# Half of a depthwise convolution moved from TensorE to VectorE, and the row maxima spread three to two over the making of the inputs

## The chip, the cores and the metric

The kernel runs on one core of a Trainium2 chip. The metric is the device time of one execution in microseconds (us), lower is better. Before the change it is 1499.34 us, the median of three runs (1496.52 to 1502.08).

## What is computed

A sequence of 2048 rows of 128 channels passes through two layers. Layer 0 is a complex exponential filter along the sequence (done as a scan) and a gated token mix. Layer 1 has a state-space block ("mamba") in two directions, forward and backward, an attention with 16 heads of 8 channels, and eight experts. The change touches the inputs of the state-space block and what lies beside their making:

```
xz = einsum('bld,ed->ble', x, Win)            # 256 channels u, 256 channels z
u, z = split(xz)
uc = depthwise_conv(u, convw, 4 taps, causal) + convb
u  = silu(uc)
dtr, Bm, Cm = split(einsum('bld,ed->ble', u, Wx))      # 8 + 16 + 16
dt = softplus(einsum('blr,dr->bld', dtr, Wdt) + bdt)
h  = exp(dt * A) * h + (dt * u) * B ;  y = h . C + u * D ;  y = (y * silu(z)) @ Wout
```

The attention is softmax(q k^T / sqrt(8)) v. The kernel takes the row maximum of the scores in a pass of its own (scores in bf16 pieces on TensorE, a maximum over each 128x512 block on VectorE), and a second pass computes the scores again, transposed and with the maximum folded in, takes the exponential on ScalarE and weighs v with it.

## The kernel before

The program has three stages with a barrier between them: `layer0_stage`, `front_stage` (queries, keys, values, the inputs of the state-space block, the whole attention) and `tail_stage` (the state-space scan, the experts). Only the front is changed, and some loads of its weights in `layer0_stage` (L140), which fetch the four taps for 256 channels.

**The chunks.** The state-space inputs are made in NN = 8 chunks n of 512 positions, four forward and four backward, each in two halves b of 128 channels. A step is one bank of PSUM written by TensorE and emptied by ScalarE; four banks (`prep`) go round. Steps are "U" (n, b), "Z" (n, b), "X" n, "D" (n, b). The order `STEPS` (L511 to L522) is: U and Z of chunks 0 and 1; then, for each pair p of chunks, U and Z of pair p+1 and X and D of pair p. A U step is four accumulating matmuls (L887) over the normed input `xm` shifted by 0 to 3 positions, each with weights W_in times a tap (`S.taps`, made once by GpSimd, L620): the convolution is inside the projection. Z is one matmul, X two (contracting u), D one with 8 rows of contraction.

**ScalarE** empties the banks in the same order (`empty`, L692): U with silu and bias to `u`, Z with silu to `z`, X as a copy to `bcx`, D as |x| to `soft` and relu to `dt`. After each pair's D steps `softened` (L719) takes exp and log1p of `soft`. Each change of function costs a table load. Then come the 256 units of the attention, two exponentials of 128x1024 each (L744).

**VectorE** makes `xm` (`normed_input`, L806; it waits for the last Z step of chunk n-2), adds the two parts of the softplus (`softplus`, L817), and takes the row maxima (`maxima`, L761: a job is two heads, so two reductions of 128x512, L768). Jobs are numbered: 32 for each of 16 attention steps. `LEAD` = 10 jobs beyond the first 32 are done before the units begin; two more jobs stand in every unit until all 512 are done. After job 31 the maxima are turned (`turn_max`, L918) and written as rows (`place_rows`, L777).

**TensorE** runs STEPS[0:16] alone (values are made after the first four), and then one step and one job's two matmuls in turn (L978 to L983), 42 times; 40 steps lie in there. The maxima's PSUM banks are a ring of three: the two matmuls of job n wait until the first reduction of job n-1 is done (L913). A unit (L984) is two scores, a job, the weighing of the unit before, a job.

**SyncE** issues all DMAs in the order of L570 to L609: the stores of the q and k pieces, `store_uz` of chunks 0 and 1 (u as soon as ScalarE has emptied it, then z), 32 loads of q and k for the first group of heads, `store_uz` 2 and 3, then for p = 0, 1: `store_bc`, `store_dt`, `store_dtu` of pair p and `store_uz` of pair p+2; then `place_max(0)` (the rows of maxima); then `store_bc`, `store_dt`, `store_dtu` of pairs 2 and 3. ScalarE may overwrite `z` of chunk n only when the store of z of chunk n-2 has landed (L703), and `bcx` of chunk n only when the store of `bcx` of chunk n-2 has landed (L707).

**GpSimd** multiplies dt by u (`scaled_input`, L623) and splits the maxima into bf16 pieces (`split_max`).

## Time and profile before

| | |
|---|---|
| median of three runs | 1499.34 us (1496.52 to 1502.08) |
| the profiled execution | 1494.55 us, of which 1492.8 us are the span of its instructions |
| TensorE, matmuls | 994.9 us busy (67%) |
| VectorE | 1241.4 us busy (83%) |
| ScalarE | 865.8 us busy (58%) |
| GpSimd | 514.5 us busy (34%) |
| granted TensorE clock, mean of the span | 0.819 of 2.4 GHz |

The span falls into five stretches: layer 0 and the making of q and k to 115.9 us; the 16 steps that TensorE makes alone to 153.9 us; steps and jobs in turn, and the log and exp of the last pair, to 261.6 us, where ScalarE starts its first attention exponential; units with jobs to 871 us, and units without to 913.4 us; the tail stage to the end.

An engine's busy share over the whole span does not say which one sets the end of a stretch. For that the rows further down give starts, durations and, in square brackets, the idle time before a group of instructions and who ended it. A matmul of 32-bit data appears as two records. Ends of matmuls are modelled, so the step from one start to the next is the better measure.

### The profile page before, as it was taken

The page shows a single profiled execution, that of the slowest core. Times are in us where ns is not written, and L with a number is a line of the kernel's source. Part 1 is how long each engine was busy: PE and PEld are TensorE (multiplying, and loading weights), DVE is VectorE, ACT ScalarE, POOL GpSimd, SP SyncE. Part 2 cuts the span into 40 slices and gives each one's busy share as a digit, 9 for nine tenths or more (in the row PEclk, how much of TensorE's full clock was granted, in tenths as well). Part 3 has the DMA queues.
Part 4 walks back from the last instruction along what each step waited for, and adds up shares of the span by engine and source line. Part 5 has one row for each costly group of instructions (what it writes and reads, how often), then busy time and mean ns, then how long its engine had stood idle before and what let it go on. Part 6 is the DMA issues. An engine that isn't in the chain of part 4 may idle for free. (4 is left out here: it accounts for less than half of the span.)

```text
span 1492.8 us, 18241 instructions
## 1 busy us (share of the span) xinstructions
PE 994.9 (67%) x5865; PEld 327.3 (22%) x5865; DVE 1241.4 (83%) x1874; ACT 865.8 (58%) x1286; POOL 514.5 (34%) x472
## 2 busy tenths in 40 slices
PE   1439997888888888888888886243275555542444
PEld 0124331111111111111111112021043333310111
DVE  7975466899999999999999932899996666798996
ACT  3134557677777777777777786243454444553441
POOL 2311021300000000000000000698995666799894
PEclk7769996899999999999999998555566767675555
DMA  3004242300000000000000003764857675795530
GB/s 88 0 3 159 107 171 107 105 13 1 1 26 26 1 1 7 21 25 2 1 1 2 1 1 73 165 134 102 199 122 172 143 171 139 169 188 112 113 85 29
DMA packets 88785, 111.42 MB, mean 75 GB/s; under 512 B 15539, under 2 KB 46042, under 8 KB 88690
## 3 DMA queue, kind: packets, MB, share of 16 engines
q1 hardware_dynamic: 87666, 108.16, 29.1%
q0 software_dynamic: 1024, 2.10, 0.5%
q8 instruction: 47, 0.77, 0.2%
q14 instruction: 48, 0.39, 0.1%
HBM read 84.36 MB, written 25.56 MB: 74 GB/s over the span
## 5 line engine op out<-in xcount | busy, mean ns | idle before, releaser
L768 DVE TENSOR_REDUCE at_mpart<-psum 128x1 f32<-128x512 f32 x1024 | 637.8, 683 | 52.5 <-PE psum L915 49.2
L744 ACT ACTIVATE at_probs<-psum 128x1024 f32<-128x1024 f32 x512 | 495.2, 1021 | 147.3 <-PE psum L943 147.0
L1276 POOL TENSOR_TENSOR t_inject<-t_dus,t_bs 128x512 f32<-128x512 f32 x256 | 320.1, 1276 | 93.3 <-issue 38.9
L1642 PE MATMUL psum<-t_hc,stack 128*32 128x512 f32 x512 | 108.2, 930 | 254.5 <-DVE t_hc L1454 254.3
L956 PE MATMUL psum<-at_probs,at_vg 128*32 128x512 f32 x2048 | 274.7, 608 | 0.5 <-ACT at_probs L744 0.4
L915 PE MATMUL psum<-at_ks,at_qs 56*128 56x512 bf16 x1024 | 203.1, 393 | 94.0 <-DVE at_mpart L768 93.3
L1334 ACT ACTIVATE psum<-t_dts,aneg 128x512 f32<-128x512 f32 x256 | 175.9, 692 | 83.5 <-DVE t_hc L1454 39.3
L640 POOL CAST at_m<-at_mneg 128x16 bf16<-128x16 f32 x16 | 3.1, 196 | 584.3 <-DVE at_mneg L773 572.7
L1531 DVE TENSOR_TENSOR_SCAN psum<-psum,t_last,t_inject 128x512 f32<-128x512 f32 x142 | 178.8, 1277 | 11.9 <-issue 9.5
L943 PE MATMUL psum<-at_qs,at_ks 59*128 59x512 bf16 x1024 | 157.8, 380 | 9.7 <-ACT at_probs L744 8.2
L915 PEld LDWEIGHTS psum<-at_ks,at_qs 56*128 56x128 bf16 x1024 | 49.3, 93 | 424.2 <-DVE at_mpart L768 408.5
L1346 ACT ACTIVATE t_last<-psum 128x1 f32<-128x1 f32 x142 | 24.2, 171 | 175.6 <-DVE t_hc L1454 175.3
L1454 DVE TENSOR_TENSOR t_hc<-psum,t_cs 128x512 f32<-128x512 f32 x186 | 124.0, 667 | 0.0
L1531 DVE TENSOR_TENSOR_SCAN t_hp<-psum,t_last,t_inject 128x512 f32<-128x512 f32 x50 | 63.4, 1269 | 36.9 <-issue 24.2
L1263 POOL TENSOR_TENSOR t_hc<-t_hp,t_cs 128x512 f32<-128x512 f32 x70 | 88.8, 1269 | 15.2 <-DVE t_hp L1531 15.1
L1642 PEld LDWEIGHTS psum<-t_hc,stack 128*32 128x32 f32 x512 | 14.5, 133 | 316.6 <-issue 300.3
L943 PEld LDWEIGHTS psum<-at_qs,at_ks 59*128 59x128 bf16 x1024 | 50.7, 96 | 60.1 <-ACT at_probs L744 30.6
L888 PE MATMUL psum<-mp_xm,mp_taps 128*128 128x512 f32 x128 | 62.9, 642 | 0.0
L626 POOL TENSOR_TENSOR mp_u<-mp_soft_dt,mp_u 128x1024 f32<-128x1024 f32 x8 | 22.2, 2798 | 107.0 <-DVE mp_soft_dt L820 107.0
L1637 PE MATMUL psum<-t_uz,diag 128*32 128x512 f32 x128 | 27.4, 946 | 45.8 <-DVE t_gated L1462 34.6
L956 PEld LDWEIGHTS psum<-at_probs,at_vg 128*32 128x32 f32 x2048 | 40.4, 108 | 60.8 <-issue 58.6
L1531 DVE TENSOR_TENSOR_SCAN psum<-psum,t_inject 128x512 f32<-128x512 f32 x44 | 52.9, 1217 | 0.6 <-ACT psum L1334 0.4
(241 smaller groups left out, 956.8 us busy)
## 6 DMA issues: line engine op xcount, KB each, us to landing
t_dts<-mp_dt_d SPq DMA_DIRECT2D x64, 256.0 KB, 6.1
t_dus<-mp_dtu_d SPq DMA_DIRECT2D x64, 256.0 KB
t_w<-in_w SPq DMA_DIRECT2D x46, 256.0 KB
t_bs<-mp_bc_d SPq DMA_DIRECT2D x128, 64.0 KB
t_cs<-mp_bc_d SPq DMA_DIRECT2D x128, 64.0 KB
mp_u_d<-mp_u SPq DMA_DIRECT2D x8, 512.0 KB, 5.1
mp_z_d<-mp_z SPq DMA_DIRECT2D x8, 512.0 KB, 4.9
mp_dt_d<-mp_soft_dt SPq DMA_DIRECT2D x8, 512.0 KB, 2.9
```

What stands on the lines that cost most here:

```text
L744: act.activation(probs[:, u_ % 2, p, :], s_pair[p], ACT.Exp, scale=float(HD) ** -0.5).then_inc(probs_ready, 1)
L768: dve.reduce_max(mpart[:, s % 2, 2 * jp + b, i, kc:kc + 1], ring[x % 3], AX.X).then_inc(ring_free, 1)
L888: mm = pe.matmul(out, S.taps[:, d, i, P * b:P * (b + 1)], xm[:, n % 2, i:i + CH], start=(i == 0), stop=(i == KC - 1))
L915: pe.matmul(ring[z_ % 3], qs[half(b, DQ), buf, of_pair(jp, c * CH + i * P, P)], ks[half(b, DQ), buf, of_pair(jp, kc * CH, CH)], start=True ...
L943: mm = pe.matmul(s_banks[p][b], ks[half(b, DM), g % 2, of_pair(p, kt * P, P)], qs[half(b, DM), g % 2, of_pair(p, c * CH, CH)], start=True, ...
L956: mm = pe.matmul(o_bank[VW * j:VW * (j + 1), :], vg[:, g % 2, kt, j, :], probs[:, u_ % 2, j // 2, CH * (j % 2):CH * (j % 2 + 1)], start=(k ...
L1263: pool.tensor_tensor(hc[:, r % 2, j, :], hp[:, by_pool[k] % NHP, :], cs[:, (NQ * (i // NB) + q) % NBC, :], ALU.mult).then_inc(pool_weighed, 1)
L1276: pool.tensor_tensor(inject[:, k % NI, :], dus[:, i % 2, j, :], bs[:, m % NBC, :], ALU.mult).then_inc(injected, 1)
L1334: act.activation(decay[k % ND], dts[:, i % 2, j, :], ACT.Exp, scale=S.aneg[:, n // NCH, m:m + 1])\
L1454: dve.tensor_tensor(hc[:, r % 2, j, :], decay[k % ND], cs[:, m % NBC, :], ALU.mult).then_inc(dve_weighed, 1)
L1531: dve.tensor_tensor_scan(h, decay[k % ND], inject[:, k % NI, :], last[:, k % PC:k % PC + 1] if n % NCH else 0.0, ALU.mult, ALU.add).then_i ...
L1642: mm = pe.matmul(y_bank[GC * j:GC * (j + 1), :], S.stack[:, :], hc[:, r % 2, j, :], start=False, stop=(q == NQ - 1), tile_position=(0, GC ...
```

## The change

- The lower 128 channels of u (half b = 0) are no longer convolved in the projection. A U step of half 0 is one matmul with the plain weights. ScalarE copies the bank to a new buffer `low` (512 + 3 columns, two chunks in turn). VectorE (`convolve`) puts the last three columns of the chunk before (or zeros) in front, multiplies by the first tap and adds the three others with fused multiply-adds, all 128x512, each waiting for the one before. ScalarE (`convolved`) then takes the silu of it in place in `u`.
- New waits: X steps and the store of u wait for that silu (`u_ready`). ScalarE's copy waits until VectorE has begun chunk n-1 and finished chunk n-2.
- Order: ScalarE takes the two silus of pair p ahead of the U and Z banks of pair p+1, and so behind `softened(p-1)`. VectorE convolves chunks 0 to 3 before the first job, and chunks 4, 5, 6, 7 behind jobs 17, 23, 37, 43. Its softplus adds stand behind jobs 14, 34 and 53 instead of 10, 23 and 36, and the inputs of chunks 6 and 7 behind job 20 instead of 14.
- `LEAD` is 28 instead of 10: 60 jobs stand ahead of the units, three beside every two steps, and 9 units fewer hold jobs. The first maxima are turned ahead of job 40 and placed behind job 39.
- The taps for half 0 are now columns of the parameter vector; the loaded and scaled taps are half as large. SyncE's order is the old one.

```diff
@@ VECS @@
+    VECS += [f"{_d}_tap{k}" for k in range(KC)]
@@ front_stage @@
-        LEAD = 10
+        LEAD = 28
+        MT_AT, OT_AT, FIRST_MT_AT = 13, 3, 40
@@ sync @@
             def store_uz(n):
                 sp.wait_ge(prep_free, USE["U", n, NB - 1] + 1)
+                sp.wait_ge(u_ready, n + 1)
@@ scalar @@
-                if k == "U":
+                if k == "U" and key[2] == 0:
+                    if n >= 2:
+                        act.wait_ge(conv_begun, n)
+                        act.wait_ge(conv_done, n - 1)
+                    act.activation(low[:, n % 2, KC - 1:], bank, ACT.Copy).then_inc(prep_free, 1)
+                elif k == "U":
...
+            def convolved(n):
+                act.wait_ge(conv_done, n + 1)
+                act.activation(u[:, n % NUS, 0, :], u[:, n % NUS, 0, :], ACT.Silu, bias=V(f"{'fb'[n // NCH]}_convb0")).then_inc(u_ready, 1)
...
             for p in range(NP):
+                convolved(2 * p)
+                convolved(2 * p + 1)
                 for key in uz_of(p + 1) if p + 1 < NP else []:
                     empty(key)
                 for key in xd_of(p):
@@ vector @@
+            def convolve(n):
+                d, c = divmod(n, NCH)
+                x, to = low[:, n % 2, :], u[:, n % NUS, 0, :]
+                if n >= NUS:
+                    dve.wait_ge(dtu_st[n - NUS], 16)
+                if n >= 2:
+                    dve.wait_ge(conv_done, n - 1)
+                if c == 0:
+                    dve.memset(x[:, 0:KC - 1], 0.0).then_inc(conv_begun, 1)
+                else:
+                    dve.wait_ge(prep_free, USE["U", n - 1, 0] + 1)
+                    dve.tensor_copy(x[:, 0:KC - 1], low[:, 1 - n % 2, CH:]).then_inc(conv_begun, 1)
+                dve.wait_ge(prep_free, USE["U", n, 0] + 1)
+                dve.wait_ge(conv_begun, n + 1)
+                dve.tensor_scalar(to, x[:, 0:CH], V(f"{'fb'[d]}_tap0"), None, ALU.mult).then_inc(tap_done, 1)
+                for i in range(1, KC):
+                    dve.wait_ge(tap_done, (KC - 1) * n + i)
+                    dve.scalar_tensor_tensor(to, x[:, i:i + CH], V(f"{'fb'[d]}_tap{i}"), to, ALU.mult, ALU.add)\
+                        .then_inc(tap_done if i < KC - 1 else conv_done, 1)
...
+            convolve(0)
             normed_input(2)
             normed_input(3)
+            convolve(1)
             dve.tensor_copy(S.identb[:, :], S.ident[:, :]).then_inc(identb_ready, 1)
+            convolve(2)
             normed_input(4)
             normed_input(5)
+            convolve(3)
             for n in range(JOBS + LEAD):
                 maxima(n)
-                if n == 10:
+                if n == 14:
                     softplus(0)
                     softplus(1)
-                if n == 14:
+                if n == 20:
                     normed_input(6)
                     normed_input(7)
-                if n == 23:
+                if n == 34:
                     softplus(2)
                     softplus(3)
-                if n == JOBS - 1:
+                if n == FIRST_MT_AT - 1:
                     place_rows(0)
-                if n == 36:
+                if n in (17, 23, 37, 43):
+                    convolve({17: 4, 23: 5, 37: 6, 43: 7}[n])
+                if n == 53:
                     softplus(4)
                     softplus(5)
@@ tensor @@
-                if k == "U":
-                    b = key[2]
+                if k == "U" and key[2] == 0:
+                    pe.wait_ge(xm_ready, n + 1)
+                    mm = pe.matmul(out, S.w_in[:, d, 0:P], xm[:, n % 2, KC - 1:], start=True, stop=True)
+                elif k == "U":
...
                 elif k == "X":
                     pe.wait_ge(prep_free, USE["U", n, NB - 1] + 1)
+                    pe.wait_ge(u_ready, n + 1)
...
             for n in range(JOBS + LEAD):
-                if n < len(beside):
-                    step(beside[n])
-                if n == JOBS:
+                if n % 3 != 2:
+                    step(beside[n - n // 3])
+                if n == FIRST_MT_AT:
                     turn_max(0)
                 maxima(n)
```

## Rows read from the trace of the kernel before

**Rows 1.** Busy by stretch: busy us (instructions) of each engine, clock, DMA, GB/s.
```profile
153.90:261.60 107.70, 97.61 (x238) 29.01 (x237) 65.26 (x99) 65.73 (x84) 17.50 (x10) 0.83 0.35 129
261.60:871.00 609.40, 518.16 (x3822) 117.11 (x3826) 592.75 (x993) 463.49 (x486) 26.00 (x69) 0.99 0.04 14
```

**Rows 2.** Waits from 115 to 265 us: us in total, times, longest.
```profile
DVE at_mpart L768 <- PE psum L915: 41.9, 22, 5.4
```

**Rows 3.** Timeline of TensorE: start us, us, instruction, count, [idle before].
```profile
115.90 7.03 PE L888 MATMUL psum<-mp_xm,mp_taps 128*128 128x512 f32 x16
...
124.49 3.73 PE L972 MATMUL psum<-w_qkv,at_vg 128*128 128x128 f32 x32
...
153.91 1.91 PE L896 MATMUL psum<-mp_u,mp_w_x 128*40 128x512 f32 x4
...
157.92 0.39 PE L915 MATMUL psum<-at_ks,at_qs 56*128 56x512 bf16 x2
158.24 1.12 PE L900 MATMUL psum<-mp_bcx,mp_w_dt 8*128 8x512 f32 x2
159.29 0.39 PE L915 MATMUL psum<-at_ks,at_qs 56*128 56x512 bf16 x2
...
164.31 6.42 PE L888 MATMUL psum<-mp_xm,mp_taps 128*128 128x512 f32 x8
...
177.69 3.70 PE L888 MATMUL psum<-mp_xm,mp_taps 128*128 128x512 f32 x8
...
250.29 2.07 PE L900 MATMUL psum<-mp_bcx,mp_w_dt 8*128 8x512 f32 x2
```

**Rows 4.** Busy, with clock, of five us in which TensorE never paused.
```profile
165.00:170.00 5.00, 5.00 (x7) 1.99 (x6) 0.71 (x2) 4.94 (x6) 0.00 (x0) 0.52 0.16 61
```

**Rows 5.** Timeline of VectorE beside the steps.
```profile
128.87 3.21 DVE L815 TENSOR_SCALAR mp_xm<-xh,vec 128x515 f32<-128x515 f32 x1
...
156.18 1.29 DVE L768 TENSOR_REDUCE at_mpart<-psum 128x1 f32<-128x512 f32 x2 [1.61 <-PE psum L915]
...
181.75 1.29 DVE L768 TENSOR_REDUCE at_mpart<-psum 128x1 f32<-128x512 f32 x2 [2.67 <-PE psum L915]
182.96 2.35 DVE L820 TENSOR_TENSOR mp_soft_dt<-mp_soft_dt 128x1024 f32<-128x1024 f32 x2
```

**Rows 6.** VectorE's groups by shape: count, busy us, mean ns, idle before.
```profile
L815 DVE TENSOR_SCALAR mp_xm<-xh,vec 128x512 f32<-128x512 f32 x2 | 1.1, 538 | 7.9 <-issue 7.9
L292 DVE TENSOR_TENSOR l_dx<-l_dx,l_xr 128x512 f32<-128x512 f32 x4 | 2.8, 693 | 0.1
L268 DVE SCALAR_TENSOR_TENSOR l_pim<-l_sin,l_sc,l_pim 128x2048 f32<-128x2048 f32 x1 | 2.4, 2352 | 0.0
```

**Rows 7.** Timeline of ScalarE: a pair's last D bank to the next silu or exponential.
```profile
198.63 0.69 ACT L716 ACTIVATE mp_soft_dt<-psum,vec 128x512 f32<-128x512 f32 x1 [0.78 <-PE psum L900]
...
207.84 0.69 ACT L700 ACTIVATE mp_u<-psum,vec 128x512 f32<-128x512 f32 x1
...
252.40 0.69 ACT L716 ACTIVATE mp_soft_dt<-psum,vec 128x512 f32<-128x512 f32 x1 [3.16 <-PE psum L900]
...
261.60 3.77 ACT L744 ACTIVATE at_probs<-psum 128x1024 f32<-128x1024 f32 x4
```

**Rows 8.** Timeline of SyncE's queue: issue of stores and of the rows of maxima.
```profile
190.24 0.47 SPq L550 DMA_DIRECT2D mp_u_d<-mp_u  x1
...
192.94 1.25 SPq L552 DMA_DIRECT2D mp_z_d<-mp_z  x1
...
233.28 3.04 SPq L541 DMA_DIRECT2D at_qs<-at_mrow  x4
```

**Rows 9.** From issue to landing, the stores of z (line 552).
```profile
DMA to landing us min/median/max: 2.8/4.9/13.3
```

**Rows 10.** Timeline of ScalarE: the last unit with jobs, then five without.
```profile
868.19 1.94 ACT L744 ACTIVATE at_probs<-psum 128x1024 f32<-128x1024 f32 x2 [0.55 <-PE psum L943]
870.68 9.57 ACT L744 ACTIVATE at_probs<-psum 128x1024 f32<-128x1024 f32 x10 [0.55 <-PE psum L943]
```

More of the change, by code:

```diff
@@ L139, in _ @@
                 for k in range(KC):
-                    sp.dma_start(S.taps[:, d, k, :], dr["taps"][d, k:k + 1, :].to_broadcast([P, DI])).then_inc(next_in, 16)
+                    sp.dma_start(S.taps[:, d, k, :], dr["taps"][d, k:k + 1, :].to_broadcast([P, P])).then_inc(next_in, 16)
                 sp.dma_start(S.w_x[:, d, :, :], dr["w_x"][d].rearrange("(b p) e -> p b e", p=P)).then_inc(next_in, 16)
@@ L426, in front_stage @@
         rden = sb("at_rden", [P, TPC, HG])
-        xm = sb("mp_xm", [P, 2, KC - 1 + CH])
+        xm, low = sb("mp_xm", [P, 2, KC - 1 + CH]), sb("mp_low", [P, 2, KC - 1 + CH])
         u, z = sb("mp_u", [P, NUS, NB, CH]), sb("mp_z", [P, 2, NB, CH])
@@ L450, in front_stage @@
         taps_ready, xm_ready = sem("mp_taps"), sem("mp_xm")
+        conv_begun, tap_done, conv_done, u_ready = sem("mp_conv_begun"), sem("mp_tap"), sem("mp_conv"), sem("mp_u_ready")
         prep_full, prep_free = sem("mp_full"), sem("mp_free")
@@ L495, in jobs_beside @@
             return [n] if n < NSTEP * JOBS else []
-        rows_at, turned_at, uses = {0: 2 * JOBS + 1}, {}, 2 * (JOBS + LEAD) + 1
+        rows_at, turned_at, uses = {0: 2 * FIRST_MT_AT + 1}, {}, 2 * (JOBS + LEAD) + 1
         for i in range(NU):
@@ L620, in scaled_taps @@
                 pool.tensor_tensor(S.taps[:, d, :, :], S.taps[:, d, :, :],
[L621 removed]
+                                   S.w_in[:, d, P:DI].unsqueeze(1).to_broadcast([P, KC, P]), ALU.mult).then_inc(taps_ready, 1)
             def scaled_input(n):
@@ L887, in step @@
                     for i in range(KC):
-                        mm = pe.matmul(out, S.taps[:, d, i, P * b:P * (b + 1)], xm[:, n % 2, i:i + CH],
+                        mm = pe.matmul(out, S.taps[:, d, i, :], xm[:, n % 2, i:i + CH],
                                        start=(i == 0), stop=(i == KC - 1))
@@ L977, in _ @@
             beside = STEPS[ALONE:]
+            assert 2 * (JOBS + LEAD) == 3 * len(beside)
             for n in range(JOBS + LEAD):
-                if n < len(beside):
-                    step(beside[n])
-                if n == JOBS:
+                if n % 3 != 2:
+                    step(beside[n - n // 3])
+                if n == FIRST_MT_AT:
                     turn_max(0)
@@ L1709, in build @@
             S.w_qkv, S.bv = sb(early, "w_qkv", [P, 3, P]), sb(early, "bv", [P, P])
-            S.w_in, S.taps = sb(early, "mp_w_in", [P, 2, 2 * DI]), sb(early, "mp_taps", [P, 2, KC, DI])
+            S.w_in, S.taps = sb(early, "mp_w_in", [P, 2, 2 * DI]), sb(early, "mp_taps", [P, 2, KC, P])
             S.w_x, S.w_dt = sb(early, "mp_w_x", [P, 2, NB, BC + DR]), sb(early, "mp_w_dt", [P, 2, DI])
@@ L1743, in pack @@
                 col[f"{d}_{n}{b}"] = a[f"L1_attn_{d}_{n}"][rows]
+        for k in range(KC):
+            col[f"{d}_tap{k}"] = a[f"L1_attn_{d}_convw"][0:P, 0, k]
     out["b1"] = a["L1_ffn_b1"].reshape(NE, NFB, P).transpose(0, 2, 1)
@@ L1756, in pack @@
         w_x.append(np.concatenate([wx[:, DR:], wx[:, :DR]], axis=1))
-        taps.append(a[f"L1_attn_{d}_convw"][:, 0, :].T)
+        taps.append(a[f"L1_attn_{d}_convw"][P:DI, 0, :].T)
         al = a[f"L1_attn_{d}_Alog"].reshape(DI // GC, GC, NS // SP4, SP4)
```

2 lines of the change are left out of this document (removed).

## The prediction

> **What bounds the kernel now.** I read the busy time by stretch first. While units hold jobs VectorE is busy 592.75 of 609.4 us [rows 1]: it sets the pace there, at 2.49 us a unit (868.19 to 870.68); without jobs ScalarE sets it, at 9.57 / 5 = 1.91 us [rows 10]. In the stretch of steps and jobs, 153.9 to 261.6, TensorE is busy 97.61 of 107.7 us at a clock of 0.83, VectorE only 65.26 [rows 1]. The waits say the same: 41.9 us in which the maxima waited for their matmuls, 22 times [rows 2]. Ahead of it, from 115.90 to 153.91, TensorE goes from step to step. So TensorE bounds 115.9 to about 250; then a chain on ScalarE (abs, relu, exp, log, tables) leads from the last D step at 250.29 to the first exponential at 261.60 [rows 3, 7]. All units, the front's end and the tail shift with that exponential. The forecast is its shift, less what the later units save.
>
> **Prices at 2.4 GHz.** A D step is 159.29 - 158.24 = 1.05 us of TensorE, a job's two matmuls 158.24 - 157.92 = 0.32, an X step 1.9, a convolved U step 3.7 [rows 3]. A lower U step becomes one matmul, two records like D: about 1.05. A job costs VectorE 1.29 us, a pair of softplus adds 2.35 [rows 5]. A convolution has one tensor-scalar of 0.54 and three multiply-adds. None of 128x512 is in the trace: a quarter of the 2352 ns one is 0.59, the two-tensor add of 128x512 takes 0.69 [rows 6]; the last is the same shape and has two SBUF inputs too. I take 0.75, as each waits for the one before, so 0.54 + 3 x 0.75 + 0.2 for the three columns = 3.0 us (bounds 2.3 to 3.2).
>
> **The lone steps: 8.5 us sooner.** TensorE loses 2.65 us in each of four chunks: 38.0 - 10.6 = 27.4 us, so X of chunk 0 could start at 143.3. VectorE's first job waits for convolution 3, which stands behind the input of chunk 5, which waits for the last lone Z step: 143.3, some 0.5 us of small waits on the way, 0.54 for the input, 3.0 for the convolution: 147.5 instead of 156.18 [rows 5], hence -8.5. (The first convolution can be stretched, as the 3.21 us of one input was [rows 5]; that has slack, the last has none.) X of chunk 0 needs a silu that is done by then. The first q and k loads follow the store of chunk 1's u, which now waits for that silu, at about 137: no later than now.
>
> **The stretch of steps and jobs.** Measured to the last D step, now 250.29 - 156.18 = 94.1 us after the first reduction. Behind it, in the new order:
> VectorE's own work up to job 57: 58 x 1.29 = 74.8, four convolutions 12.0, three pairs of softplus adds 7.1, inputs and small ones 1.4; less 2 us by which TensorE is ahead: 93.3 us. TensorE's work for the whole stretch is only 60 x 0.32 + 8 x 1.9 + 16 x 1.05 + 8 x 1.05 + 4 x 1.05 + 4 x 3.7 = 78.6 us. So VectorE would bind, and the two would take as long as now. But three things keep it from being fed.
> 1. *The ring is short.* The matmuls of a job are issued when the first reduction of the job before is done, so VectorE has three reductions, 1.9 us, in hand while TensorE makes one step. Beside a 3.7 us step, with the job's matmul and its latency 4.4, it runs dry for 2.5 us; the trace has 2.67 us idle there now [rows 5]. Four such steps lie beside jobs: 10.0. Two X steps in a row leave it dry for about 0.7 + 0.9 = 1.6: three times 4.8. No convolution or softplus add stands behind job 9, 15, 30 or 36, where it would cover the gap.
> 2. *A ring between three engines before X of chunk 6.* Its silu stands on ScalarE behind the log of pair 2, so behind the last D step of chunk 5 (job 49). Bank to next silu takes 207.84 - 198.63 = 9.2 us [rows 7]; with 1.4 from the step's start and 0.7 for the silu that is 11.3 us, while TensorE has only two jobs to do and VectorE is done after 3 to 4. It stands idle for 8.5 us less what it has in hand. Then the copy of X of chunk 6 into bcx waits for the store of bcx of chunk 4, and SyncE issues that behind the stores of u and z of 6 and 7 (190.24 to 194.2 now, 3.9 us), which now wait for the silus, and behind the four of the maxima (3.04) [rows 8]; landing adds 2.8 to 4.9 [rows 9]. D of chunk 6 then starts 10.7 us after X, not 5.2; a softplus add covers part of it, 3.5 remain. Together 12.0 (bounds 8 to 18).
> 3. *The clock.* It fell to 0.52 while TensorE was busy 5.00 of 5 us [rows 4], behind a run of D steps (8 rows of contraction), and a U step behind it took 6.42 instead of 3.70 [rows 3]. The new order has longer runs of D and jobs, 7.7 instead of 5.5 us each, and then an idle TensorE. I put 2.5 for each of two D runs and 3 for what follows the idle: 8.0 (bounds 0 to 16).
> Sum: 93.3 + 10.0 + 4.8 + 12.0 + 8.0 = 128.1 us against 94.1: +34.0. With -8.5 the last D step comes 25.5 us later, near 276; the chain behind it (11.3 us) is the same. ScalarE's eight copies and silus more (10 us) lie where it waits for banks, except the two counted.
>
> On the clock the Trainium skill, "TensorE: Matmul & The Clock Gate", Part 1, speaks of a busy monitor: an engine that is kept busy gets its full clock, and only idle time throttles it. The trace disagrees: 0.52 with no idle time at all [rows 4]. By the page alone only the idle behind job 50 would cost anything, and the sum would be 5 us less.
>
> **The units.** 18 jobs are gone from them: 9 units at 1.91 instead of 2.49 us [rows 10]: -5.2. GpSimd's split of the first maxima gets eight jobs of time; TensorE's wait there, under 2 us, is inside the noise of the sum. The store waits of z (chunks 4 and 6 wait for z of 2 and 4, stored late now) take ScalarE 4 to 5 us each, with four banks in front of TensorE: nothing, and 3 us each if that cover is gone. Layer 0 loads 0.5 MB less of broadcast taps under other work: nothing.
>
> **The sum.** +25.5 - 5.2 = +20.3 us. The profiled execution, 1494.55 us (span 1492.8), would be 1514.9; it lies 4.8 below the median, so the median goes from 1499.34 to 1519.6. I say 1519.
>
> **The rivals.**
> - *VectorE is fed after all (ends on the other side: no slower).* If the jobs that three-for-two spacing puts between steps keep the ring full, terms 1 and 3 vanish and the ring of engines costs its least: 93.3 + 8 = 101.3 against 94.1, +7.2 - 8.5 - 5.2 = -6.5: 1493. For it: TensorE has 20 us less to do than VectorE. Against: the 2.67 us idle beside a job that precedes a 3.7 us step; the ring is three banks in either kernel. It decides at the gap behind jobs 9, 15, 30 and 36: under 1 us there and this rival holds. With the lone steps 3 us sooner than I have them, it goes to 1490.
> - *The clock stays low.* If TensorE is at 1.2 GHz for most of the stretch, a D step and a job cost 2.5 us (250.29 is such a step, 2.07 long [rows 3]), more than VectorE's 1.29, and VectorE starves all along: about 16 us more than forecast: 1535. For it: TensorE would be waiting for the maxima much of the time. Against: beside the units it waits for them as well and holds 0.99 [rows 1].
> - *The stores bind more.* If z of chunks 2 and 4 land as late as the latest of now (13.3 us [rows 9]), ScalarE frees the banks late and TensorE stands twice for some 4 us more: 1527.
> - *The change doesn't do what it says.* If a lower U step took as long as before (it reads the same input), the lone steps would be 10.6 us later and the rest 10: above 1535; two records for one matmul in D speak against it.
>
> **How the numbers follow.** Forecast 0.58, fed 0.17, low clock 0.12, stores 0.11, not as said 0.02. Bounds of the terms that do not go together: from 8 + 0 below (-12) to +14 above, so the forecast's own range is 1508 to 1532. With part of the fed case outside and most of the slow ones in, 8 in 10 lie in 1503 to 1535. About 0.5% (7.5 us) is what a measurement can tell from no change. Faster by more needs the fed case and an early start: 0.05. Within: the rest of the fed case, and a forecast whose terms all come small: 0.15. Slower: 0.80.
>
> **What would show it.** The first reduction near 147.5; gaps of 2 to 3 us on VectorE behind jobs 9, 15, 30, 36; about 8 us of idle on TensorE and VectorE behind job 50, ended by ScalarE's in-place silu; then a copy to bcx that waits for a DMA; the first exponential near 287 instead of 261.6; 30 units at 1.91 us. Wrong if the first exponential comes before 270: then term 1 or 2 has a cover that I do not see. Wrong the other way if the clock is at 0.5 before job 40.

## The result and the profile after

The changed kernel takes 1535.77 us (median of four runs, 1532.57 to 1537.76) against 1498.91 us of the kernel before on the same chip: ratio 1.0243 (1.0216 to 1.0269), 36.9 us slower. The direction was forecast, the size was not: 1519 was said, and the result lies just above the range of 1503 to 1535. The profiled execution took 1537.76 us, with a span of 1536.0, which is 43.2 us more than the profiled execution of before.

A slip ahead of the prediction: the kernel before loads q and k for the first group with 24 DMAs (12 and 12), not 32. No number rests on it.

I cut the span at the same marks in both kernels (us). The last D step has two records; the mark is the start of the second, 1.0 us behind the start of the step (0.5 us at full clock):

| | before | after | difference |
|---|---|---|---|
| start to first reduction | 156.2 | 150.9 | -5.3 |
| first reduction to the last D step (second record) | 95.1 | 143.2 | +48.1 |
| last D step to first exponential | 10.3 | 10.3 | 0.0 |
| units | 651.8 | 646.5 | -5.3 |
| tail (same code in both) | 579.4 | 585.1 | +5.7 |

The tail moves by itself: over the thirteen profiled executions of this study it took 579.4 to 585.6 us with the same code. The marks before it say what the change did: about 37.5 us later at the tail's start, as the medians do.

The busy times by stretch answer to [rows 1] (TensorE, its weight loads, VectorE, ScalarE, GpSimd, then clock, DMA share, GB/s). The stretches are the lone steps, four pieces of the stretch of steps and jobs, and, from a second answer, that stretch from the first reduction to the start of the last D step:

```profile
111.70:141.00 29.30, 27.95 (x90) 13.89 (x88) 23.04 (x41) 15.20 (x24) 5.95 (x4) 1.00 0.50 173
150.90:192.90 42.00, 33.95 (x80) 9.34 (x80) 30.08 (x47) 19.14 (x26) 5.56 (x2) 0.78 0.32 121
192.90:245.40 52.50, 39.61 (x89) 11.02 (x87) 35.79 (x59) 19.84 (x27) 6.33 (x6) 0.73 0.23 83
245.40:276.20 30.80, 17.56 (x36) 3.73 (x34) 15.68 (x26) 14.89 (x19) 0.00 (x0) 0.61 0.00 0
276.20:304.40 28.20, 18.68 (x42) 3.98 (x42) 16.26 (x24) 14.52 (x18) 5.56 (x2) 0.62 0.44 159
...
150.94:293.11 142.17, 104.54 (x230) 26.86 (x230) 91.37 (x144) 58.45 (x79) 17.45 (x10) 0.72 0.25 93
```

In the last line neither engine is full: VectorE is busy 91.37 of 142.17 us, TensorE 104.54, at a clock of 0.72. In the kernel before TensorE was busy 90.39 of the 95 us of this stretch (the line stands further down). It is busy for longer now, though at full clock the change took about 5 us of work from it: four convolutions less (2.65 us each), 18 jobs more (0.32 us each).

VectorE is idle for 50.8 us of the stretch. From 111 to 305 us its reductions waited 55.0 us for their matmuls, against the 41.9 of [rows 2] (115 to 265 us):

```profile
DVE at_mpart L783 <- PE psum L959: 55.0, 26, 11.0
```

**Ahead of the lone steps.** The front's first operations on VectorE and GpSimd, in the kernel before and then in the one after:

```profile
99.46 8.00 DVE L823 TENSOR_SCALAR at_vg<-xh,vec 128x512 f32<-128x512 f32 x4 [7.11 <-PEq L59]
...
101.18 4.62 POOL L620 TENSOR_TENSOR mp_taps<-mp_taps,mp_w_in 128x1024 f32<-128x1024 f32 x2
```
```profile
100.92 5.30 DVE L858 TENSOR_SCALAR at_vg<-xh,vec 128x512 f32<-128x512 f32 x4 [7.47 <-PEq L60]
...
102.64 2.83 POOL L624 TENSOR_TENSOR mp_taps<-mp_taps,mp_w_in 128x512 f32<-128x512 f32 x2
```

GpSimd scales half as many taps, 2.83 instead of 4.62 us, and VectorE's four inputs of q and k beside it take 5.30 instead of 8.00 us. The first of the four alone takes 2.04 instead of 6.63 us, and TensorE starts its first projection when it is done (103.00 and 106.15).

**The lone steps.** TensorE comes to them 4.2 us sooner than before, at 111.69 instead of 115.90, though the stage began 1.5 us later. X of chunk 0 starts at 140.99. Then (timeline of TensorE, and of SyncE's queue):

```profile
140.99 1.91 PE L940 MATMUL psum<-mp_u,mp_w_x 128*40 128x512 f32 x4
150.29 0.61 PE L959 MATMUL psum<-at_ks,at_qs 56*128 56x512 bf16 x2 [7.39 <-DMA at_ks<-k_parts]
```
```profile
133.95 0.77 SPq L534 DMA_DIRECT2D at_qs<-q_parts  x1
...
141.97 0.28 SPq L536 DMA_DIRECT2D at_ks<-k_parts  x1
...
149.44 0.28 SPq L536 DMA_DIRECT2D at_ks<-k_parts  x1
```

The first job's matmuls wait 7.39 us for a load of k. SyncE needs 8.3 us to issue the first 12 of the 24 loads (133.95 to 142.25), and begins only behind the stores of u and z of chunks 0 and 1. The job starts 8.0 us behind the issue of the twelfth.

**VectorE beside the steps.** Its timeline, only groups that waited (this answers to [rows 5]):

```profile
150.94 1.29 DVE L783 TENSOR_REDUCE at_mpart<-psum 128x1 f32<-128x512 f32 x2 [6.25 <-PE psum L959]
...
174.69 6.41 DVE L783 TENSOR_REDUCE at_mpart<-psum 128x1 f32<-128x512 f32 x10 [3.64 <-PE psum L959]
185.12 2.49 DVE L783 TENSOR_REDUCE at_mpart<-psum 128x1 f32<-128x512 f32 x4 [0.55 <-PE psum L959]
...
221.64 1.29 DVE L783 TENSOR_REDUCE at_mpart<-psum 128x1 f32<-128x512 f32 x2 [4.47 <-PE psum L959]
235.78 1.29 DVE L783 TENSOR_REDUCE at_mpart<-psum 128x1 f32<-128x512 f32 x2 [3.99 <-PE psum L959]
...
280.45 1.29 DVE L783 TENSOR_REDUCE at_mpart<-psum 128x1 f32<-128x512 f32 x2 [11.03 <-PE psum L959]
```

Groups 2 to 5 stand beside the four steps that are still convolved on TensorE, the last one in the ring of three engines. Not shown are eleven gaps of 1.25 us, nine between these lines and two behind the last, each beside a step at the slow clock.

**The clock.** TensorE's timeline, D steps and jobs, the steps behind a convolution of VectorE, and the ring:

```profile
160.11 0.61 PE L959 MATMUL psum<-at_ks,at_qs 56*128 56x512 bf16 x2 [0.78 <-ACT mp_soft_dt L726]
160.64 2.07 PE L944 MATMUL psum<-mp_bcx,mp_w_dt 8*128 8x512 f32 x2
...
163.18 2.07 PE L944 MATMUL psum<-mp_bcx,mp_w_dt 8*128 8x512 f32 x2
...
191.24 0.39 PE L959 MATMUL psum<-at_ks,at_qs 56*128 56x512 bf16 x2 [2.55 <-DVE at_mpart L783]
192.44 0.61 PE L959 MATMUL psum<-at_ks,at_qs 56*128 56x512 bf16 x2 [0.81 <-DVE at_mpart L783]
192.98 3.17 PE L940 MATMUL psum<-mp_u,mp_w_x 128*40 128x512 f32 x4
...
204.84 0.61 PE L959 MATMUL psum<-at_ks,at_qs 56*128 56x512 bf16 x2 [2.61 <-DVE at_mpart L783]
...
264.10 2.07 PE L944 MATMUL psum<-mp_bcx,mp_w_dt 8*128 8x512 f32 x2
...
276.27 3.60 PE L940 MATMUL psum<-mp_u,mp_w_x 128*40 128x512 f32 x4 [8.18 <-ACT mp_u L730]
...
285.81 1.09 PE L944 MATMUL psum<-mp_bcx,mp_w_dt 8*128 8x512 f32 x2 [1.81 <-ACT mp_bcx L717]
```

From 160.64 a D step and a job's matmuls take 2.54 us (163.18 - 160.64) instead of 1.37: the slow level, 1.2 GHz. The matmuls of job 0, behind the wait for the loads, are at that level already (0.61 us at 150.29), and the D run falls back to it at job 4. So the prediction's "wrong the other way if the clock is at 0.5 before job 40" came true at once. A mean clock of 0.72 between levels of 0.5 and 1 means that 56% of the stretch is at the slow level.

**The ring.** The silus that TensorE waited for, the copy to bcx behind them (ScalarE), and SyncE's issues in between:

```profile
275.41 1.33 ACT L730 ACTIVATE mp_u<-mp_u,vec 128x512 f32<-128x512 f32 x2
285.08 1.07 ACT L717 ACTIVATE mp_bcx<-psum 40x512 f32<-40x512 f32 x2 [8.34 <-DMA mp_bc_d<-mp_bcx]
```
```profile
278.04 1.24 SPq L556 DMA_DIRECT2D mp_z_d<-mp_z  x1
279.32 3.94 SPq L544 DMA_DIRECT2D at_qs<-at_mrow  x4
283.30 0.87 SPq L560 DMA_DIRECT2D mp_bc_d<-mp_bcx  x2
```

X of chunk 6 starts 12.2 us behind the last D step of chunk 5, D of chunk 6 9.5 us behind X. Meanwhile no DMA moves from 245.4 to 276.2 (share 0.00 in the fourth stretch above): SyncE's order holds every store behind u of chunk 6.

**The units without jobs** run at 22.78 / 12 = 1.90 us (two exponentials each), as in [rows 10]:

```profile
926.96 22.78 ACT L759 ACTIVATE at_probs<-psum 128x1024 f32<-128x1024 f32 x24 [0.48 <-PE psum L987]
```

### The profile page after: what moved, and what is told of

Its sections match the earlier page's. It is cut to its first block and busy times, and to the rows that moved or that the text cites. A ratio compares the mean times of both kernels' runs of the same rounds, so it can differ in the third digit from the quotient of the medians.

```text
span 1536.0 us, 18219 instructions
## 1 busy us (share of the span) xinstructions
PE 995.1 (65%) x5817; PEld 320.1 (21%) x5817; DVE 1260.3 (82%) x1914; ACT 869.2 (57%) x1295; POOL 511.5 (33%) x472
## 5 line engine op out<-in xcount | busy, mean ns | idle before, releaser
L959 PE MATMUL psum<-at_ks,at_qs 56*128 56x512 bf16 x1024 | 208.0, 403 | 123.5 <-DVE at_mpart L783 112.3
L1576 DVE TENSOR_TENSOR_SCAN t_hp<-psum,t_inject 128x512 f32<-128x512 f32 x20 | 24.2, 1212 | 32.5 <-POOL t_inject L1321 19.9
```

The costliest lines, as they stand in the source:

```text
L959: pe.matmul(ring[z_ % 3], qs[half(b, DQ), buf, of_pair(jp, c * CH + i * P, P)], ks[half(b, DQ), buf, of_pair(jp, kc * CH, CH)], start=True ...
L1576: dve.tensor_tensor_scan(h, decay[k % ND], inject[:, k % NI, :], last[:, k % PC:k % PC + 1] if n % NCH else 0.0, ALU.mult, ALU.add).then_i ...
```

## The experiments

Each is compared with the kernel before on its own chip (1496.99, 1495.71 or 1494.82 us). "Stretch" is from the first reduction to the last D step, by the mark above: 95.1 before, 143.2 after. One caution on the first exponentials: the front's first operation starts at 100.92 in the change, and at 98.66 to 100.68 in runs with the same code ahead of it. Up to 2.3 us of a "sooner" come from there and not from the edit.

| | edit | median | ratio (95%) | first reduction | stretch | first exp |
|---|---|---|---|---|---|---|
| jobs_only | 60 jobs, no convolution on VectorE | 1514.20 | 1.0114 (1.0087 to 1.0141) | 155.1 | 118.6 | 284.1 |
| conv_only | convolution, 42 jobs | 1513.84 | 1.0111 (1.0084 to 1.0137) | 150.9 | 116.1 | 277.3 |
| silu_early | after, silus ahead of softened | 1528.64 | 1.0206 (1.0184 to 1.0229) | 149.5 | 136.8 | 296.6 |
| dfull_after | after, D over 128 rows | 1522.55 | 1.0178 (1.0158 to 1.0197) | 149.2 | 130.2 | 289.2 |
| loads_first | after, q and k loads first | 1525.04 | 1.0209 (1.0182 to 1.0235) | 145.6 | 141.5 | 297.4 |
| align | after, convolutions behind 15, 30, 36, 43 | 1526.85 | 1.0213 (1.0193 to 1.0233) | 148.7 | 138.2 | 297.2 |
| mended_long | after, all of these but dfull, and two more | 1518.03 | 1.0156 (1.0129 to 1.0183) | 145.4 | 131.9 | 287.7 |
| mended_short | the same on conv_only | 1500.87 | 1.0040 (1.0025 to 1.0055) | 145.7 | 108.3 | 264.3 |
| before_pad | before, D over 128 rows | 1487.08 | 0.9943 (0.9925 to 0.9961) | 156.1 | 86.7 | 252.6 |
| mended_2 | mended_short, two convolutions sooner | 1498.86 | 1.0031 (1.0017 to 1.0045) | 145.9 | 105.8 | 261.9 |
| mended_2_pad | mended_2, D over 128 rows | 1487.75 | 0.9948 (0.9931 to 0.9966) | 147.7 | 94.1 | 252.2 |

### The two halves of the change

```diff
@@ jobs_only: from before @@
-        LEAD = 10
+        LEAD = 28
...
-        MT_AT, OT_AT = 13, 3
+        MT_AT, OT_AT, FIRST_MT_AT = 13, 3, 40
...
-                if n < len(beside):
-                    step(beside[n])
+                if n % 3 != 2:
+                    step(beside[n - n // 3])
@@ conv_only: from after @@
-        LEAD = 28
+        LEAD = 10
...
-        MT_AT, OT_AT, FIRST_MT_AT = 13, 3, 40
+        MT_AT, OT_AT, FIRST_MT_AT = 13, 3, 32
...
-                if n in (17, 23, 37, 43):
-                    convolve({17: 4, 23: 5, 37: 6, 43: 7}[n])
+                if n in (11, 15, 25, 29):
+                    convolve({11: 4, 15: 5, 25: 6, 29: 7}[n])
...
-                if n % 3 != 2:
-                    step(beside[n - n // 3])
+                if n < len(beside):
+                    step(beside[n])
```

The softplus adds and the inputs of chunks 6 and 7 go with the spread of the jobs: jobs_only has them at the new places, conv_only at the old ones.

> The kernel before with only the new spread of jobs (60 jobs ahead of the units, three beside two steps, first maxima turned ahead of job 40, softplus adds behind jobs 14, 34, 53); the convolution stays on TensorE. Theory 1 (VectorE is starved by the three-bank ring beside long steps, and longer runs of D steps and jobs put TensorE at 1.2 GHz): the last D step comes about 112 us after the first reduction instead of 94, the units save 5.2: about 1511. Rival (the engines' sums of work decide, order and clock do not): TensorE's sum grows by 18 x 0.32 = 5.8 us, less 5.2: 1499, no change.

> The changed kernel with the old spread (42 jobs ahead of the units, one beside each step; convolutions of chunks 4 to 7 behind jobs 11, 15, 25, 29). Theory 1: TensorE has 10.6 us less beside the jobs and starts its jobs about 5 us sooner, but X of chunk 6 waits for the silu behind the log of pair 2 (about 8 us of idle) and its copy for the store of bcx; last D step 104 us after the first reduction: about 1503. Rival (sums decide): 42 jobs, four convolutions and the adds are 74.6 us of VectorE, TensorE's sum 72.8: first exponential 15 us sooner than in the kernel before, 1484.

Measured: the stretch grows by 23.5 us with the jobs alone and by 21.0 with the convolution alone (44.5 together, 48.1 in the change). In medians 17.2 and 16.9 us, 34.1 together against 36.9. So the parts nearly add up, and both were under-estimated: to the start of the last D step 112 and 104 us were expected, 117.6 and 115.1 measured. Neither half is a gain that the other spoils. The convolution alone has the whole ring of three engines: its TensorE timeline has

```profile
249.71 3.60 PE L940 MATMUL psum<-mp_u,mp_w_x 128*40 128x512 f32 x4 [9.56 <-ACT mp_u L730]
...
259.24 1.17 PE L944 MATMUL psum<-mp_bcx,mp_w_dt 8*128 8x512 f32 x2 [3.43 <-ACT mp_bcx L717]
```

and with fewer jobs to do in the meantime TensorE waits 9.56 + 3.43 us there, against 8.18 + 1.81 in the change.

The clock separates the two halves. The stretch of jobs_only, then that of conv_only:

```profile
155.10:273.80 118.70, 101.85 (x255) 29.75 (x255) 80.92 (x126) 55.72 (x74) 17.46 (x10) 0.85 0.29 107
...
150.90:267.00 116.10, 88.67 (x193) 23.96 (x193) 71.06 (x108) 59.13 (x80) 15.66 (x10) 0.76 0.30 109
```

With the longer runs of D steps and jobs alone the clock is 0.85, as good as the 0.86 of before. With the convolution on VectorE it is 0.76 (0.81 ahead of the ring, to 239 us), and with both 0.72. So the longer runs, which the prediction's clock term was mostly about, hardly lower the clock by themselves. Whether TensorE's waits behind the convolutions do it, or the loss of 128-row matmuls from its work, no run separates.

### The ring: silus ahead of softened

```diff
-                convolved(2 * p)
-                convolved(2 * p + 1)
+                if p == 0:
+                    convolved(0)
+                    convolved(1)
                 for key in uz_of(p + 1) if p + 1 < NP else []:
                     empty(key)
                 for key in xd_of(p):
                     empty(key)
+                if p + 1 < NP:
+                    convolved(2 * p + 2)
+                    convolved(2 * p + 3)
                 softened(p)
```

> The changed kernel with one edit: ScalarE takes the two in-place silus of pair p+1 ahead of the exp and log of pair p. Theory 1: the 11.0 us idle of VectorE before job 51 shrinks to under 4, the 8.3 us wait of the bcx copy for its DMA goes, one table load less: first exponential 11 to 15 us sooner than the 304.4 of the changed kernel, about 1523. Rival (VectorE's sum of 60 jobs and four convolutions is the bound): the idle moves elsewhere, within 3 us of 1536.

Measured: 7.8 us sooner at the first exponential instead of 11 to 15, 1.4 of it ahead of the first reduction. VectorE's idle time before job 51, 11.03 us, is 2.25:

```profile
270.21 1.29 DVE L787 TENSOR_REDUCE at_mpart<-psum 128x1 f32<-128x512 f32 x2 [2.25 <-PE psum L963]
```

The silu's place on ScalarE is the cause of that idle time. But D of chunk 6 still starts 9.5 us behind X (266.77 to 276.31): the copy to bcx now stands behind exp and log on ScalarE, and then waits for its DMA for 1.72 us more. The ring's second half turned into another wait of the same length.

### The clock: D steps over 128 rows

```diff
-                    mm = pe.matmul(out, S.w_dt[BC:BC + DR, d, P * b:P * (b + 1)], bcx[BC:BC + DR, n % 2, :], start=True, stop=True)
+                    mm = pe.matmul(out, S.w_in[:, d, P * b:P * (b + 1)], u[:, n % NUS, 1, :], start=True, stop=True)
```

> The changed kernel, but the D steps multiply 128 rows (other weights, and the upper half of u) instead of 8; dt is therefore a different number and the output is not the reference's. Same count and size of matmuls otherwise. Theory 1 (runs of 8-row matmuls with jobs bring the clock down though TensorE is busy): the granted clock from 150.9 us to the idle behind job 50 is above 0.95 instead of 0.78 and 0.73, and the first exponential comes 10 to 16 us sooner, about 1523. Rival (it is TensorE's waiting for VectorE that brings it down): clock and time stay within 3 us of 1536.

Measured: the stretch is 13.0 us shorter, the first exponential 15.2 us sooner, and TensorE is busy 92 instead of 105 us with as many matmuls. The line for the stretch up to 0.5 us ahead of the last D step:

```profile
149.20:278.40 129.20, 91.54 (x227) 23.93 (x227) 90.18 (x144) 58.01 (x78) 16.04 (x10) 0.82 0.27 98
```

The clock is 0.82 instead of 0.72: more than the 8.0 us that I gave the clock lies in the D steps alone. It is still not full, though above 0.95 was expected. The D step keeps its waits, and VectorE's idle time before job 51 is 11.03 us here too, so the ring is intact.

### The loads of q and k

```diff
-            both(store_uz, 0)
             for w in range(2):
                 sp.wait_ge(stored[w], 16 * NCH)
-            for j in range(HG):
-                load(0, j)
+            load(0, 0)
+            load(0, 1)
+            both(store_uz, 0)
+            load(0, 2)
+            load(0, 3)
```

> The changed kernel with one edit: SyncE issues the 12 loads of q and k for the first two heads ahead of the stores of u and z of chunks 0 and 1 (the other 12 behind them). Theory 1 (the first job waits 7.4 us for these loads, because they are issued behind a store that now waits for the in-place silu of chunk 1, and TensorE falls to 1.2 GHz in that wait): the first reduction comes at about 145 instead of 150.9, bound by convolution 3, the first D steps run at full clock; first exponential 7 to 10 us sooner, about 1527. Rival (the loads are bound by the landing of the k pieces, not by their place in the queue): first job within 2 us of 150, time unchanged.

Measured: the first reduction comes at 145.6 instead of 150.9, and the first exponential 7.0 us sooner (5.3 there, 1.7 in the stretch). TensorE starts its first job right behind X of chunk 0 (143.81). Of the 7.0 us 1.6 lie ahead of the front; against that TensorE now waits 2.35 us for ScalarE ahead of X of chunk 0, and ScalarE 6.99 us for the landing of a store of z that stands behind the loads. The distance of the median to the kernel before shrinks by 7.5 us. So the late loads cost 5 to 7 us, a wait that was nowhere in my sum. The first D steps were expected at full clock, but the second of them (149.26) is at the slow level, with no wait of TensorE above 0.81 us behind X of chunk 0.

### Convolutions where the ring runs dry

```diff
-                if n in (17, 23, 37, 43):
-                    convolve({17: 4, 23: 5, 37: 6, 43: 7}[n])
+                if n in (15, 30, 36, 43):
+                    convolve({15: 4, 30: 5, 36: 6, 43: 7}[n])
```

> The changed kernel with convolutions 4, 5, 6, 7 behind jobs 15, 30, 36, 43 instead of 17, 23, 37, 43: three of them lie just ahead of a 3.7 us U step. Theory 1 (VectorE runs dry beside each long step, since the ring holds 1.9 us of reductions, and TensorE runs dry during each convolution): the gaps of VectorE behind jobs 15, 30, 36 vanish, and so do TensorE's 2.8 us waits behind jobs 17, 23, 37; the last D step 7 to 10 us sooner than in the changed kernel, about 1527. Rival (VectorE's sum is the bound and its gaps are only moved): within 3 us of 1536.

Measured: the stretch is 4.9 us shorter; 7 to 10 were expected. VectorE's own work can fill the gaps beside the convolved steps, as the prediction's first term says. But convolution 4 now follows the softplus adds and runs beside GpSimd's product, and TensorE waits 5.75 us behind them (188.42).

### All mends together, with 60 and with 42 jobs

mended_long has the three edits above (silus, loads, positions), and ScalarE takes the two X banks of the last pair ahead of the log of pair 2, and SyncE stores bcx of pair 2 ahead of u and z of pair 3. mended_short puts the same on conv_only, with convolutions behind jobs 10, 20, 24, 28.

```diff
-                for key in xd_of(p):
+                for key in xd_of(p)[2 if p == NP - 1 else 0:]:
                     empty(key)
...
+                if p == NP - 2:
+                    for key in xd_of(p + 1)[:2]:
+                        empty(key)
                 softened(p)
@@ sync @@
                 both(store_dtu, p)
+                if p == 1:
+                    both(store_bc, 2)
                 both(store_uz, p + 2)
```

> The changed kernel with all orders mended: silus ahead of exp and log, loads first, convolutions aligned with the long steps, and besides X of chunks 6 and 7 emptied by ScalarE ahead of the exp and log of pair 2, with the store of bcx of pair 2 ahead of the stores of u and z of pair 3. Theory 1 (the loss is the sum of waits and of the clock behind them): 8 + 9 + 9 + 6 us come back, about 1505, still above the kernel before, since 60 jobs and four convolutions are 96 us of VectorE where the kernel before needed 94.1 in all. Rival (VectorE plus clock stay the bound): not below 1518.

> The same mended orders with the old spread of jobs (42 ahead of the units, one beside each step; convolutions behind jobs 10, 20, 24, 28). Theory 1: from the 1514 of the short spread 25 us come back, so that TensorE's 10 us less beside the jobs and the lone steps' 8 us show at last: 1485 to 1493. Rival (the lower load lets the clock fall and takes it back): 1498 or more.

Measured: 1518.03 and 1500.87 us, both slower than expected, by 13 us and by 8 or more. 8 + 9 + 9 + 6 us were to come back in mended_long. In the distance of the median to the kernel before, its three single edits gave 5.2, 7.5 and 5.7 us (18.5 in sum), and all five together 14.5. With intervals of about 3 us either way 14.5 and 18.5 can't be told apart, but 14.5 is half of what was expected. The waits come back elsewhere. TensorE stands 5.74, 2.79 and 5.51 us behind VectorE's convolutions and softplus adds and 2.87 us behind ScalarE's copy to `low`, and its clock over the stretch is 0.74. In mended_short the worst one stands behind this piece of VectorE's timeline, with GpSimd's product of the same time under it:

```profile
168.98 1.22 DVE L867 TENSOR_TENSOR mp_soft_dt<-mp_soft_dt 128x1024 f32<-128x1024 f32 x1
170.14 0.06 DVE L852 MEMSET mp_low<- 128x3 f32 x1
170.33 2.36 DVE L858 TENSOR_SCALAR mp_u<-mp_low,vec 128x512 f32<-128x512 f32 x1
172.72 4.28 DVE L861 SCALAR_TENSOR_TENSOR mp_u<-mp_low,vec,mp_u 128x512 f32<-128x512 f32 x3
```
```profile
169.14 5.74 POOL L635 TENSOR_TENSOR mp_u<-mp_soft_dt,mp_u 128x1024 f32<-128x1024 f32 x2 [42.88 <-DVE mp_soft_dt L867]
```

A convolution that takes 0.49 + 2.33 us elsewhere takes 2.36 + 4.28 here, and TensorE waits 6.05 us for the reductions behind it.

### What the clock costs by itself

before_pad is the kernel before with D steps over 128 rows. In the weights the 8 rows stand among 120 rows of zeros; in bcx the 32 rows of B and C, which meet zero weights, stand ahead of them, and the 88 rows behind are cleared.

```diff
+            pool.memset(S.w_dt[:, :, :], 0.0).then_inc(wdt_clear, 1)
...
-        bcx = sb("mp_bcx", [BC + DR, 2, CH])
+        bcx = sb("mp_bcx", [P, 2, CH])
...
+            pool.memset(bcx[:, :, :], 0.0).then_inc(bcx_clear, 1)
...
-                    mm = pe.matmul(out, S.w_dt[BC:BC + DR, d, P * b:P * (b + 1)], bcx[BC:BC + DR, n % 2, :], start=True, stop=True)
+                    mm = pe.matmul(out, S.w_dt[:, d, P * b:P * (b + 1)], bcx[:, n % 2, :], start=True, stop=True)
```

> The kernel before with one thing changed: the D steps contract over 128 rows (the 8 rows of the step among 120 rows of zeros, in weights and in bcx), so its outputs are the same numbers. Theory (the runs of 8-row D steps lower TensorE's clock, with no idle time needed): the mean clock of the stretch of steps and jobs rises from 0.83 to 0.92 or more, no step in it shows the slow level behind a D run, and the stretch from the first reduction to the last D step is 6 to 9 us shorter than 95: a median 5 to 8 us below the kernel before. Rival (the clock follows idle time only, or D steps do not set it): clock 0.83, the same slow steps, within 2 us of before.

Measured: 1487.08 against 1494.82 us, 0.9943 (0.9925 to 0.9961), with the stretch at 86.7 instead of 95.1. The same 95 us of both kernels, before first (the padded kernel is past its last D step at 243.4):

```profile
156.00:251.00 95.00, 90.39 (x218) 27.75 (x217) 57.57 (x87) 55.88 (x74) 14.91 (x9) 0.86 0.33 123
```
```profile
156.00:251.00 95.00, 83.94 (x233) 25.91 (x231) 64.26 (x98) 62.73 (x82) 17.52 (x10) 0.97 0.37 137
```

The clock goes from 0.86 to 0.97. Where [rows 3] have a D step followed by a convolved step of 6.42 us, the padded kernel has

```profile
162.34 1.12 PE L904 MATMUL psum<-mp_bcx,mp_w_dt 128*128 128x512 f32 x2
163.40 0.39 PE L919 MATMUL psum<-at_ks,at_qs 56*128 56x512 bf16 x2
163.71 3.70 PE L892 MATMUL psum<-mp_xm,mp_taps 128*128 128x512 f32 x8
```

One thing was changed, in a stretch without a convolution on VectorE and nearly without idle time on TensorE. So it is the 8-row matmuls that lower the clock there, and this costs the kernel before 8 us.

### The rest with and without low clock

mended_2 is mended_short with convolution 4 behind job 8, ahead of the softplus adds that set GpSimd going, and convolution 5 behind job 13. mended_2_pad adds the padding.

```diff
-                if n in (10, 20, 24, 28):
-                    convolve({10: 4, 20: 5, 24: 6, 28: 7}[n])
+                if n in (8, 13, 24, 28):
+                    convolve({8: 4, 13: 5, 24: 6, 28: 7}[n])
```

> The 42-job version with all mends, with the convolution of chunk 4 behind job 8 instead of 10 (ahead of the softplus adds, so that it does not run beside GpSimd's product) and that of chunk 5 behind job 13 instead of 20. Theory (the two longest waits of TensorE there, 6.05 us behind softplus and the stretched convolution and 4.64 us for the copy of the lower bank of chunk 6, are made by these two positions): both waits fall under 2 us, the first convolution takes 2.9 us instead of 6.9, and the stretch falls from 108 to 98 to 101: 1491 to 1495, slightly below the kernel before. Rival (the waits only move, since TensorE and VectorE share a ring of three banks and each 3 us job of VectorE stops TensorE and lowers its clock): 1498 to 1502, clock in 150 to 250 still below 0.8.

> The version above with D steps over 128 rows. Theory: clock above 0.9 from the first reduction to the last D step, another 6 to 10 us: 1483 to 1488, faster than the kernel before and than the padded kernel before. Rival (the waits of TensorE behind each convolution lower the clock by themselves): clock between 0.8 and 0.87, 2 to 4 us less than the version without padding, and not below the padded kernel before.

Measured: 1498.86 and 1487.75 us. In mended_2 convolution 4 takes 0.49 + 2.33 us as expected, and the 6.05 us wait is gone. But convolution 6 now meets GpSimd's product of the next pair (VectorE's timeline, and GpSimd's):

```profile
206.98 1.11 DVE L855 COPY mp_low<-mp_low 128x3 f32<-128x3 f32 x1
208.20 2.45 DVE L858 TENSOR_SCALAR mp_u<-mp_low,vec 128x512 f32<-128x512 f32 x1
210.69 2.33 DVE L861 SCALAR_TENSOR_TENSOR mp_u<-mp_low,vec,mp_u 128x512 f32<-128x512 f32 x3
```
```profile
204.81 5.56 POOL L635 TENSOR_TENSOR mp_u<-mp_soft_dt,mp_u 128x1024 f32<-128x1024 f32 x2 [27.44 <-DVE mp_soft_dt L867]
```

TensorE waits 5.01 us there. The rival's number holds: 1498 to 1502. The padding is worth 11.1 us, the stretch goes from 105.8 to 94.1, and its clock goes from 0.76 to 0.91:

```profile
145.90:251.60 105.70, 86.75 (x189) 24.20 (x189) 71.29 (x109) 57.62 (x79) 15.18 (x10) 0.76 0.32 117
```
```profile
147.70:241.80 94.10, 75.02 (x190) 22.38 (x189) 71.32 (x109) 57.87 (x79) 15.18 (x9) 0.91 0.36 131
```

With 75.02 us of TensorE's and 71.32 of VectorE's work in 94.1 us, it ends level with the padded kernel before (1487.75 against 1487.08), and not below it as expected. Its first reduction comes 8.4 us sooner, its stretch is 7.4 us longer: VectorE's convolution only moves the time. No kernel of the study is faster than the padded one of before.

## Why the prediction was wrong in size

The forecast shift of the profiled execution was +20.3 us, the measured one +43.2. The 22.9 between them: the stretch 14.1 (128.1 forecast to the start of the last D step, 142.2 measured), the first reduction 3.3 (147.7 to 150.9), the tail 5.7, and the units -0.1. The tail is the spread of its own; in medians 16.6 us were missed.

**Lone steps, -8.5: two terms missed, of both signs.** They took 29.3 us where 27.4 were forecast, but began 4.2 us sooner: I had costed the halved taps at nothing in layer 0, and not looked at their scaling by GpSimd in the front, beside which VectorE's inputs take 8.00 us. X of chunk 0 came at 140.99, 2.3 us sooner than the 143.3 forecast, and the last convolution ahead of the jobs took 0.49 + 2.33 us and 0.16 for the columns: the 3.0 of the sum. Convolution 3 ends at 144.7, and the first reduction should have followed at once; it does in loads_first (145.6). I wrote that the loads come "no later than now" and compared their start with before; what had moved was the time by which they are needed: behind X of chunk 0, 140.99 instead of 153.91. Issuing 12 loads takes 8.3 us, and the first job starts another 8.0 us behind the last of them. The step failed for pricing neither.

**VectorE's work, 93.3: measured 91.4.** Three multiply-adds took 2.33 us, 0.78 each with their waits, against 0.75.

**The short ring.** Four gaps of 2.5 us were forecast beside the convolved steps. In dfull_after, where the clock is high there, they are 2.67, 0.55, 2.67 and 2.64: the mechanism and the size are right, one of the four being covered by the softplus adds behind job 14. Two X steps: 9.2 us there (2.53, 1.90 + 0.88, 2.81 + 1.12) instead of 4.8, since the first pair starts from an empty ring and the others behind a wait at a low clock.

**The ring of three engines, 12.0: right.** 12.2 us from D to X (11.3 forecast), 9.5 from X to D (10.7), and 11.03 us of VectorE's idle time and 1.12 behind it: 12.2. silu_early shows that the silu's place makes the first half.

**The clock, 8.0 with bounds 0 and 16: this is the step that failed.** To the start of the last D step the 8-row D steps alone cost 12.5 us (142.2 against 129.6). In dfull_after three gaps of 1.25 and two of 0.8 to 0.95 us beside steps at the slow level are left, 5.5 us. So the clock costs about 18 us, 10 more than the sum has and above its upper bound. Two errors made it. I looked for the loss where a D run is longer than before, which costs little by itself (0.85 in jobs_only), and not for what the kernel before already pays: 8.0 us to the start of the last D step (94.1 against 86.1 in before_pad), which my 94.1 contained and my new sum, built up from VectorE's 93.3, did not. And I counted 3 us for one idle stretch, while each of the four convolutions stops TensorE as well (2.55, 2.61, 2.79, 2.79 us) with slow steps behind it: 3.17 us at 192.98 for an X step of 1.91, 2.07 at 257.63 for a D step of 1.12. Slow steps stand behind these four waits in dfull_after too, which has no 8-row matmul.

The remaining 9.5 us between dfull_after (129.6) and my sum without its clock term (120.1) are: X steps +4.4, slow steps left +5.5, the turn of the maxima on TensorE +1.3, small waits between reductions +2.3, the covered gap -1.5, VectorE's work -2.6 (90.65 us to the start of the last D step), the ring +0.1. So of the 14.1 us by which the stretch was missed the clock term is 10 and the X steps are 4.4, some of it at the slow level too.

**The units, -5.2: measured -5.3.** The chain behind the last D step was the same. The z stores made ScalarE wait 5.9 us and cost nothing visible, as said.

**The rivals.** "The clock stays low" had a chance of 0.12, gave 1535 and came closest: TensorE is at the slow level for 56% of the stretch, the "most" that it asks for. I held against it that TensorE keeps 0.99 beside the units while it waits for maxima; but the units' scores have 59 rows of contraction and the D steps 8, and [rows 4] had shown 0.52 beside those. "VectorE is fed" fell at 3.64 us idle behind job 9; the rival on stores had no part.

The Trainium skill ("TensorE: Matmul & The Clock Gate", Part 1) has the clock fall when the engine is idle. before_pad speaks against that as the only cause here: with the same steps in the same order, more rows alone raised it from 0.86 to 0.97 in the same 95 us. What idle time adds can't be separated cleanly: TensorE's waits in mended_2_pad leave 0.91, those of dfull_after 0.82.

## What to carry to other kernels

Work taken from a busy engine is a gain only if its new place doesn't stop that engine: here each 3 us job of VectorE stops TensorE behind a ring of three banks, and what the lone steps gain the stretch behind them gives back. When a step starts sooner, price every transfer it needs from the time it is needed, not from its old start. And when a sum is built up anew instead of from the old duration, put in what the old duration had already paid for, such as a low clock.

A matmul with few rows of contraction is worth filling with zeros where the granted clock drops beside it: it cost two clears and nothing in the loop, and gave 7.7 us here.

## What was unexpected of the hardware

- The rows of contraction alone move TensorE's clock: 8 to 128 rows raised it from 0.86 to 0.97 over 95 us in one kernel, from 0.72 to 0.82 and from 0.76 to 0.91 in two others. The same step's duration at full clock is the same (1.12 us for 8 and for 128 rows).
- VectorE's operations between SBUF tensors that begin during a GpSimd product end just behind it, or behind its first half, 0.03 to 0.6 us later in these rows. In mended_short the two halves of the product end at 172.40 and 174.88: a tensor-scalar of 128x512 takes 2.36 instead of 0.49 us and ends at 172.69, and the first multiply-add takes 2.71 instead of 0.75 and ends at 175.43. In mended_2 they end at 208.07 and 210.37: the copy of three columns takes 1.11 instead of 0.16 us and ends at 208.10, the tensor-scalar takes 2.45 and ends at 210.65, and the multiply-adds behind it, begun at 210.69, take their usual 2.33. Reductions from PSUM keep 0.68 us beside the product (205.78 in mended_2). The Trainium skill ("GPSIMD Engine Reference", 1. Specifications) says that GpSimd shares its SBUF interfaces with VectorE; how long VectorE is held is in these rows.
- Mending single waits of a ring gave half of what the waits had promised: 14.5 us instead of 32, since others of 5.74 and 5.51 us came in their place.
